# Linear attention layer: both batches in one program without a barrier, steps alternating on TensorE

## The chip, the cores and the metric

The program runs on one core of a Trainium2 chip. The metric is the device time of one execution in microseconds (us), lower is better. Three runs of the kernel before gave 1944.12, 1944.92 and 1945.78; their median is 1944.92 us. TensorE does the matrix products, VectorE (DVE) and ScalarE (ACT) the work on rows, GpSimd (POOL) and SyncE (SP) the rest. The engines run each its own list of instructions in order and wait for one another on semaphores only. Matmul results land in PSUM, which has eight banks of 512 float32 columns.

## The reference, cut to what matters

The program is a decoder of two blocks, six layers in all, on x of 2 x 1024 x 256 (batches, tokens, features). The change touches the first layer alone, linear attention with its feed-forward part. With 4 heads of 64 features it computes, for each batch by itself:

```
h1 = (x - mean) / sqrt(var + eps)                # a norm without gain
h2 = layer_norm(h1, ln1_g, ln1_b)                # a norm of the normed
q, k, v = h2 @ wq, h2 @ wk, h2 @ wv
q = softmax(q * scale) over the 64 features of a head
k = softmax(k * scale) over the 1024 tokens
context = k^T v  (64 x 64 for each head)
y = (q context) @ wo + bo + h1
y = gelu(layer_norm(y, ln2_g, ln2_b) @ w_ff1 + b_ff1) @ w_ff2 + b_ff2 + y
x = x + y @ w_d + b_d
```

All of it is in float32. w_ff1 is 256 x 1024 and w_ff2 1024 x 256, so these two hold half of the layer's products.

## The kernel before, in words

x lies in SBUF with features on partitions: two tiles of 128 features (k or m = 0, 1) and, for a batch, two halves of 512 tokens (j = 0, 1). `linear_attention_layer` runs a loop over the batches, `nc.Fori(0, B)` (L330), whose body is one block of four engine programs (L334). The block ends with a barrier of all engines. Both passes use the same `c.arena` of six slots, the same eight banks and the same semaphores, whose counts go on from pass to pass.

The order of work in a pass is written out by hand, as a list for each engine. TensorE (L349 on): the norm's mean and variance (`layer_norm_pe`: products with a matrix of 1/256), keys (L355, banks 0 to 3), values (L361, banks 4 to 7), queries (L368), the turned keys (transposes, L376), the contexts (L383), the turned queries (L390), attend (L397), the output projection (L403), the second norm, widening (L414, four banks in turn), narrowing (L422) and the last product (L430). ScalarE squares, takes logarithms and exponentials for the norm (`layer_norm_act`), the exponentials of keys (L440) and queries (L444), copies turned tiles out of PSUM (L447, L451, L456) and computes the gelu (L464). VectorE centres and scales (`layer_norm_dve`: L181, L185, L195, L201, L206), takes maxima of keys (L474), copies values (L481), shifts queries by their maximum (L487, L489), divides them by their sum (L493 to L497), copies the contexts (L508) and adds residuals (L514, L522, L528).

SyncE starts a transfer of one of two pieces of the later layers' weights in each pass (L340). After the loop `clear_signals` (L288) clears each semaphore of the layer on GpSimd, in a block of its own; `wait_for_weights` (L2372) is another, and then the next layer begins with the additions of L260.

Of the kernel before, what the change touches and what calls it, by code (L numbers as in the profile page):

```python
# [24 lines left out]
ALU = mybir.AluOpType  # L25
# [3 lines left out]
P = 128  # L29
B, S, D = 2, 1024, 256  # L30
T = B * S
FT = D // P
# [109 lines left out]
def layer_norm_pe(pe, c, s):  # L142

    for j in range(NCH):
        pe.wait_ge(*s["ln_sum"](j + 1))
        pe.matmul(c.bank(j), c.mean_w[:], c.ln_s[:, j, :], start=True, stop=True).then_inc(s["ln_mean"].sem)
    for j in range(NCH):
        pe.wait_ge(*s["ln_sq"](j + 1))
        for k in range(FT):
            mm = pe.matmul(c.bank(2 + j), c.mean_w[:], c.slot(3)[:, k, j * CH:(j + 1) * CH],  # L150
                           start=(k == 0), stop=(k == FT - 1))
        mm.then_inc(s["ln_var"].sem)


def layer_norm_act(act, c, s, twice=False):

    for j in range(NCH):  # L160
        act.wait_ge(*s["ln_cent"](j + 1))
        act.activation(c.slot(3)[:, :, j * CH:(j + 1) * CH], c.slot(2)[:, :, j * CH:(j + 1) * CH],
                       ACT.Square).then_inc(s["ln_sq"].sem)
    for j in range(NCH):
        act.wait_ge(*s["ln_var"](j + 1))
        ins = act.activation(c.ln_d[:, j, :], c.bank(2 + j), ACT.Ln, bias=c.eps[:, 0:1])
        if twice:
            ins = act.activation(c.ln_s[:, j, :], c.bank(2 + j), ACT.Ln, bias=c.eps_eps[:, 0:1], scale=1.0 + LN_EPS)
        ins.then_inc(s["ln_log"].sem)
    for j in range(NCH):  # L170
        act.wait_ge(*s["ln_log"](j + 1))
        ins = act.activation(c.ln_r[:, j, :], c.ln_d[:, j, :], ACT.Exp, scale=-0.5)
        if twice:
            ins = act.activation(c.ln_s[:, j, :], c.ln_s[:, j, :], ACT.Exp, scale=-0.5)
        ins.then_inc(s["ln_rstd"].sem)


def layer_norm_dve(dve, c, s, x, out, gain=None, bias=None, twice=False, once_out=None):

    for j in range(NCH):  # L180
        dve.tensor_tensor(c.ln_s[:, j, :], x(0, j), x(1, j), ALU.add).then_inc(s["ln_sum"].sem)  # L181
    for j in range(NCH):
        dve.wait_ge(*s["ln_mean"](j + 1))
        for k in range(FT):
            ins = dve.tensor_tensor(c.slot(2)[:, k, j * CH:(j + 1) * CH], x(k, j), c.bank(j), ALU.subtract)  # L185
        ins.then_inc(s["ln_cent"].sem)
    factor = c.ln_s if twice else c.ln_r
    for j in range(NCH):
        dve.wait_ge(*s["ln_rstd"](j + 1))
        centred = lambda k: c.slot(2)[:, k, j * CH:(j + 1) * CH]  # L190
        for k in range(FT):
            if gain is None:
                ins = dve.tensor_tensor(out(k, j), centred(k), factor[:, j, :], ALU.mult)
            else:
                ins = dve.scalar_tensor_tensor(out=out(k, j), in0=centred(k), scalar=gain(k), in1=factor[:, j, :],  # L195
                                               op0=ALU.mult, op1=ALU.mult)
                ins.then_inc(s["ln_scaled"].sem)
        if gain is not None:
            for k in range(FT):
                dve.wait_ge(*s["ln_scaled"](FT * j + k + 1))  # L200
                ins = dve.tensor_scalar(out(k, j), out(k, j), bias(k), None, ALU.add)  # L201
        if once_out is None or j < NCH - 1:
            ins.then_inc(s["ln_out"].sem)
        if once_out is not None:
            for k in range(FT):
                ins = dve.tensor_tensor(once_out(k, j), centred(k), c.ln_r[:, j, :], ALU.mult)  # L206
            if j == NCH - 1:
                ins.then_inc(s["ln_out"].sem)


LN_SIGNALS = {"ln_sum": NCH, "ln_mean": NCH, "ln_cent": NCH, "ln_sq": NCH, "ln_var": NCH, "ln_log": NCH, "ln_rstd": NCH,
              "ln_scaled": FT * NCH, "ln_out": NCH}
# [88 lines left out]
def linear_attention_layer(nc, c):  # L301

    DH = 64
    SCALE = float(DH) ** -0.25
    with ExitStack() as ctx:
        s = signals(nc, ctx, "a", dict(
            LN_SIGNALS, k_proj=4, k_max=4, k_shift=1, k_max_all=1, k_added=1, k_inv=1, zeroed=1, k_exp=4, k_turned=4, k_copied=4, v_proj=4, v_copied=4,
            q_proj=4, q_max=4, q_shift=4, q_exp=4, q_sum=4, q_inv=4, q_norm=4, q_turned=4, q_copied=4,
            ctx_done=1, ctx_copied=1, at_done=4, at_copied=4, o_done=4, y_done=4,
            ff_done=16, ff_gelu=16, f2_done=4, y2_done=4, d_done=4, x_done=4))  # L310
        s2 = signals(nc, ctx, "a2", LN_SIGNALS)
        sb = lambda name, shape: ctx.enter_context(nc.sbuf_tensor(name, shape, F32))
        k_mx = sb("a_k_mx", [P, FT, NCH])
        k_m = sb("a_k_m", [P, FT])
        k_s = sb("a_k_s", [P, FT, NCH])
        k_r = sb("a_k_r", [P, FT])
        q_m = sb("a_q_m", [P, 4, 8])
        q_s = sb("a_q_s", [P, 4, 8])
        context = sb("a_context", [P, FT, P])
        h1, h2, ek, v, ekt, qn = (c.slot(i) for i in range(6))  # L320
        v_t = v.rearrange("p a n -> p (a n)").rearrange("p (t n) -> p t n", t=TT)
        ekt_t = ekt.rearrange("p a n -> p (a n)").rearrange("p (t n) -> p t n", t=TT)
        q_t = qn.rearrange("p a n -> p (a n)").rearrange("p (u n) -> p u n", u=4)
        qt, at = c.slot(2), c.slot(5)
        y = h1
        hid = [c.arena[:, (2 + 2 * j) * 2048:(4 + 2 * j) * 2048].rearrange("p (f n) -> p f n", f=8) for j in range(NCH)]
# [3 lines left out]
        with nc.Fori(0, B) as b:  # L330
            set_round(b, s, s2)
            x = lambda k, j: c.xT[:, k, bass.ds(b * S + j * CH, CH)]
            col = lambda t: (lambda k, j: t[:, k, j * CH:(j + 1) * CH])
            with nc.Block() as block:  # L334

                @block.sync
                def _(sync):

                    sync.wait_ge(c.first_loaded, 32)
                    sync.dma_start(c.weights[:, bass.ds(b * part + n_first, part)],  # L340
                                   c.weights_dram[:, bass.ds(b * part + n_first, part)]).then_inc(c.others_loaded, 16)

                @block.gpsimd
                def _(pool):
                    pool.memset(context[:], 0.0).then_inc(s["zeroed"].sem)

                @block.tensor
                def _(pe):
                    layer_norm_pe(pe, c, s)  # L349
                    pe.wait_ge(c.first_loaded, 32)  # L350
                    pe.wait_ge(*s["ln_out"](NCH))
                    for m in range(FT):
                        for j in range(NCH):
                            for k in range(FT):
                                mm = pe.matmul(c.bank(2 * m + j), c.w("a_wk", k, m * P, P), h2[:, k, j * CH:(j + 1) * CH],  # L355
                                               start=(k == 0), stop=(k == 1))
                            mm.then_inc(s["k_proj"].sem)
                    for u in range(4):
                        for t in (0, 1):
                            for k in range(FT):  # L360
                                mm = pe.matmul(c.bank(4 + u)[:, t * D:(t + 1) * D], h2[:, k, (2 * u + t) * P:(2 * u + t + 1) * P],  # L361
                                               c.w("a_wv", k, 0, D), start=(k == 0), stop=(k == 1))
                        mm.then_inc(s["v_proj"].sem)
                    for u in range(4):
                        pe.wait_ge(*s["v_copied"](u + 1))
                        for t in (0, 1):
                            for k in range(FT):
                                mm = pe.matmul(c.bank(4 + u)[:, t * D:(t + 1) * D], h2[:, k, (2 * u + t) * P:(2 * u + t + 1) * P],  # L368
                                               c.w("a_wq", k, 0, D), start=(k == 0), stop=(k == 1))
                        mm.then_inc(s["q_proj"].sem)  # L370

                    pe.wait_ge(*s["k_exp"](4))
                    for u in range(4):
                        for t in (0, 1):
                            for m in range(FT):
                                mm = pe.transpose(c.bank(u)[:, t * D + m * P:t * D + (m + 1) * P],  # L376
                                                  ek[:, m, (2 * u + t) * P:(2 * u + t + 1) * P], c.ident[:])
                        mm.then_inc(s["k_turned"].sem)
# [29 lines left out]
                    for j in range(NCH):  # L408
                        pe.wait_ge(*s2["ln_out"](NCH))
                        for f in range(8):  # L410
                            if n >= 4:
                                pe.wait_ge(*s["ff_gelu"](n - 3))
# [2042 lines left out]
```

## Time and profile before

| what | value |
|---|---|
| median of three runs | 1944.92 us |
| the profiled execution | 1944.75 us |
| its span, first to last instruction | 1943.0 us |
| mean granted TensorE clock | 0.938 |
| TensorE, VectorE, ScalarE busy | 1688.1, 941.2, 625.1 us |
| first pass of the layer, from the first addition to the second pass's | 7.7 to 155.9 us |
| second pass, to the last addition | 155.9 to 301.8 us |
| next layer's first addition | 306.95 us |

The rows further down come from the one profiled execution. A float32 matmul with 512 columns shows as two records, so 64 records of L414 are 32 matmuls. A row of a timeline may merge several instructions in succession ("x8"); its second number is then the time from the first's start to the last's end. The granted clock is 1.0 at 2.4 GHz and 0.5 at 1.2 GHz.

### The profile page before, as it was taken

The numbers are of one execution on the slowest core, as the hardware profiler recorded it, in microseconds if no ns is written. First come the engines' busy times: TensorE is split into PE (matmuls) and PEld (weight loads), VectorE is DVE, ScalarE is ACT, GpSimd is POOL, SyncE is SP. The second block draws the span as 40 slices with busy tenths as digits, with TensorE's granted clock in tenths as the row PEclk, the third lists the DMA queues.
The fourth block names the chain that finished last, engine by engine and source line by source line (L and its number), as shares of the span: only waits on it lengthen the run. The fifth ranks groups of instructions, "written<-read, shape, count | busy, mean of one in ns | idle before, by whom it ended". The sixth has DMA issues, their size and how long they took to land. (4 is left out here: it accounts for less than half of the span.)

```text
span 1943.0 us, 19762 instructions
## 1 busy us (share of the span) xinstructions
PE 1688.1 (87%) x7458; PEld 955.6 (49%) x7458; DVE 941.2 (48%) x1490; ACT 625.1 (32%) x1024; POOL 119.4 (6%) x92
## 2 busy tenths in 40 slices
PE   5796795989999958977799999778767999999998
PEld 3443442543222213333444544345553888888886
DVE  3404404567656541133587775355545536353542
ACT  2312322432232231114166666242242222221220
POOL 0000000001121200003500000000011000000000
PEclk8898897989999979988899999899968999999999
DMA  4001000000000000002724520000111022222211
GB/s 174 0 0 59 0 0 4 0 1 1 1 1 1 1 1 0 0 0 76 87 82 52 67 34 2 3 1 0 52 36 58 1 87 87 87 87 87 87 30 44
DMA packets 27693, 67.47 MB, mean 35 GB/s; under 512 B 3096, under 2 KB 14424, under 8 KB 25176
## 3 DMA queue, kind: packets, MB, share of 16 engines
q1 hardware_dynamic: 27608, 66.33, 12.5%
q8 instruction: 54, 0.88, 0.2%
q14 instruction: 31, 0.25, 0.0%
HBM read 57.80 MB, written 8.39 MB: 34 GB/s over the span
## 5 line engine op out<-in xcount | busy, mean ns | idle before, releaser
L1566 ACT ACTIVATE arena<-psum 128x512 f32<-128x512 f32 (+3 forms) x384 | 164.3, 499 | 123.6 <-PE psum L1470 91.6
L1606 DVE TENSOR_REDUCE b_mx<-psum 128x1 f32<-128x512 f32 (+3 forms) x304 | 181.5, 653 | 45.0 <-PE psum L1448 34.4
L2100 PE MATMUL psum<-m_wo,m_hidden 128*128 128x256 f32 (+1 forms) x704 | 153.4, 379 | 1.0 <-DVE arena L2303 1.0
L2198 ACT ACTIVATE m_gelu<-psum 128x512 f32<-128x512 f32 (+1 forms) x88 | 52.6, 598 | 305.1 <-PE psum L2086 305.1
L2100 PEld LDWEIGHTS psum<-m_wo,m_hidden 128*128 128x128 f32 (+1 forms) x704 | 133.3, 190 | 19.7 <-issue 1.2
L2086 PE MATMUL psum<-m_x_high,m_w_high 128*128 128x512 f32 (+1 forms) x352 | 139.9, 398 | 2.9 <-issue 2.9
L2086 PE MATMUL psum<-m_x_rest,m_w_high 128*128 128x512 f32 (+1 forms) x352 | 138.8, 394 | 0.0
L2086 PE MATMUL psum<-m_x_high,m_w_rest 128*128 128x512 f32 (+1 forms) x352 | 138.4, 393 | 0.0
L2322 DVE TENSOR_TENSOR m_hidden<-m_gelu,psum 128x512 f32<-128x512 f32 (+1 forms) x88 | 60.5, 688 | 139.8 <-PE psum L2086 139.8
L878 ACT ACTIVATE x_probs<-psum 128x1024 f32<-128x1024 f32 x64 | 65.5, 1024 | 179.4 <-PE psum L734 179.4
L954 DVE TENSOR_REDUCE x_mx<-psum 128x2 f32<-128x1024 f32 x64 | 77.4, 1222 | 83.6 <-PE psum L708 82.4
L1467 PE MATMUL psum<-b_q_stack,b_k_stack 98*128 98x512 bf16 (+3 forms) x288 | 91.4, 334 | 7.4 <-DMA b_q_stack<-b_stage 3.0
L1445 PE MATMUL psum<-b_k_stack,b_q_stack 96*128 96x512 bf16 (+3 forms) x288 | 90.2, 345 | 6.0 <-POOL weights_sb L1395 3.7
L747 PE MATMUL psum<-x_probs,arena 128*64 128x512 f32 x256 | 69.5, 621 | 6.8 <-ACT x_out L888 6.8
L2086 PEld LDWEIGHTS psum<-m_x_high,m_w_high 128*128 128x128 f32 (+1 forms) x352 | 65.0, 185 | 19.9 <-issue 3.7
L734 PE MATMUL psum<-arena 64*128 64x512 f32 x256 | 73.7, 653 | 0.0
L2086 PEld LDWEIGHTS psum<-m_x_high,m_w_rest 128*128 128x128 f32 (+1 forms) x352 | 65.0, 185 | 16.5
L2086 PEld LDWEIGHTS psum<-m_x_rest,m_w_high 128*128 128x128 f32 (+1 forms) x352 | 65.0, 185 | 16.3
L1482 PE MATMUL psum<-arena,weights_sb 128*32 128x512 f32 (+3 forms) x768 | 71.7, 492 | 0.0
L414 PE MATMUL psum<-arena,weights_sb 128*128 128x512 f32 x128 | 58.5, 620 | 14.2 <-DVE arena L201 14.2
L708 PE MATMUL psum<-arena 64*128 64x512 f32 x256 | 68.1, 623 | 3.1 <-DVE x_mx L954 1.9
L1132 PE MATMUL psum<-weights_sb 128*128 x96 | 48.9, 634 | 18.1 <-PEq L1110 12.2
(372 smaller groups left out, 2730.8 us busy)
## 6 DMA issues: line engine op xcount, KB each, us to landing
m_w<-w SPq DMA_DIRECT2D x16, 1368.0 KB, 8.9
m_wo<-wo SPq DMA_DIRECT2D x8, 1280.0 KB
weights_sb<-weights SPq DMA_DIRECT2D x2, 2820.0 KB, 8.9
b_q_stack<-b_q_dram SPq DMA_DIRECT2D x36, 128.0 KB, 6.9
b_k_stack<-b_k_dram SPq DMA_DIRECT2D x36, 128.0 KB, 7.4
weights_sb<-weights SPq DMA_DIRECT2D x1, 3328.0 KB, 13.0
b_q_dram<-b_q_parts SPq DMA_DIRECT2D x6, 512.0 KB, 3.3
b_k_dram<-b_k_parts SPq DMA_DIRECT2D x6, 512.0 KB, 4.4
```

The costliest lines, as they stand in the source:

```text
L708: mm = pe.matmul(to[:, h * CH:(h + 1) * CH], qt[b][rows, m, q0:q0 + P], kt_[b][rows, m, first:first + CH], start=True, stop=True)
L734: mm = pe.matmul(to[0:keys, h, :], k, qt[b][rows, m, half * CH:(half + 1) * CH], start=False, stop=True)
L747: mm = pe.matmul(out_tile[h * DH:(h + 1) * DH, :], v, probs[slot % RING][0:keys, h, :], start=(kt == 0), stop=(kt == TT))
L878: ins = act.activation(probs[slot % RING][:], two_heads(units), ACT.Exp, scale=SCALE)
L954: dve.tensor_reduce(mx[:, n % 2, i // 2, i % 2, :], two_heads(tile(("piece", n, i))), AX, ALU.max).then_inc(s["read"].sem)
L1445: mm = pe.matmul(bank[:, x * keys:(x + 1) * keys], qs[n % 3][0:ROWS, h, qi * P:(qi + 1) * P], ks[n % 3][0:ROWS, h, first:first + keys], st ...
L1467: mm = pe.matmul(score(slot)[:, 0:n], ks[a][0:ROWS + SHIFT, h, ki * P:(ki + 1) * P], qs[a][0:ROWS + SHIFT, h, q0:q0 + n], start=True, stop ...
L1482: mm = pe.matmul(out_tile[h * PAD:(h + 1) * PAD, CH - n:CH], v_aug[:, b * TT + ki, quad * QUAD + h, :], probs[(QUAD * (2 * pair + i) + h) ...
L1566: act.activation(probs[slot % RING][:, 0:n], score(slot)[:, 0:n], ACT.Exp, scale=SCALE).then_inc(s["expd"].sem)
L1606: dve.tensor_reduce(mx[:, part, qi, heads[0]:heads[0] + nh], tile(("piece", p))[:, 0:nh * keys].rearrange("p (h n) -> p h n", n=keys), AX, ...
L2086: mm = pe.matmul(c.bank(base + n % 2)[0:H_N(h), :], of[:, k, at], x_of[:, k, :], start=(k == 0 and of is w_high[w] and x_of is x_high), st ...
L2100: mm = pe.matmul(bank[:, q * D:(q + 1) * D], hidden[0:H_N(h), h, (2 * i + q) * P:(2 * i + q + 1) * P], wo[0:H_N(h), h, :], start=(h == 0), ...
```

## The change

The loop goes. The Python code writes both batches into one block, with no barrier between them. Batch b has semaphores, an arena (a second one of 48 KB per partition is added), small tables and four banks of its own (4b to 4b + 3). The three layer norm helpers go; their steps become small functions of the batch, as do all others. Each engine's program is a list of such steps in which the batches alternate. Within the steps:

- The first norm's factor that h2 needs is exponentiated first; the other (`once`) has its own signal, and h1 is computed after h2. The keys start once the first half of h2 is there.
- With four banks, values and queries use the keys' banks: values wait for the exponentials of the keys, the turned keys for the shifted queries. The turned queries have three banks in turn, since the fourth holds the contexts; the widening has two in turn.
- Projection, second norm and narrowing go half by half of the tokens.
- SyncE starts both pieces of weights at once. The clears go over the semaphores of both batches.

The core of the diff (steps with the same body as before are left out):

```diff
-        with nc.Fori(0, B) as b:
-            set_round(b, s, s2)
...
+        arenas = (c.arena, sb("a_arena", [P, 6 * FT * S]))
...
+        bank = lambda b, i: c.bank(4 * b + i)
+        turn_bank = lambda b, u: bank(b, u % 3)
...
+                for i in range(B):
+                    at_i = slice(n_first + i * part, n_first + (i + 1) * part)
+                    sync.dma_start(c.weights[:, at_i], c.weights_dram[:, at_i]).then_inc(c.others_loaded, 16)
...
+                def by_token(b, name, free, done):
+                    for u in range(4):
+                        pe.wait_ge(*free(u + 1))
...
+                def turn_queries(b):
+                    for u in range(4):
+                        pe.wait_ge(*sg[b]["q_norm"](u + 1))
+                        if u == 3:
+                            pe.wait_ge(*sg[b]["q_copied"](1))
...
+                def widen(b, j):
+                    pe.wait_ge(*ln2[b]["out"](j + 1))
+                    for f in range(8):
+                        if f >= 2:
+                            pe.wait_ge(*sg[b]["ff_gelu"](8 * j + f - 1))
...
+                def narrow(b, j):
+                    pe.wait_ge(*sg[b]["ff_gelu"](8 * (j + 1)))
...
-        clear_signals(nc, s, s2)
+        clear_signals(nc, *ln1, *ln2, *sg, also=[zeroed])
```

The three lists, one step after another (in the diff each is one line of code, `ln1`, `ln2` the two norms' signals):

```
TensorE: mean(0, ln1) variance(0, ln1) [first weights] keys(0) mean(1, ln1) values(0)
  variance(1, ln1) queries(0) keys(1) turn_keys(0) values(1) contexts(0) queries(1)
  turn_queries(0) attend(0) turn_keys(1) project(0) contexts(1) turn_queries(1)
  mean(0, ln2) attend(1) variance(0, ln2) project(1) widen(0, 0) mean(1, ln2) widen(0, 1)
  variance(1, ln2) narrow(0, 0) widen(1, 0) narrow(0, 1) last(0, 0) widen(1, 1) last(0, 1)
  narrow(1, 0) narrow(1, 1) last(1, 0) last(1, 1)
ScalarE: square(0) roots_twice(0) exp_keys(0) square(1) roots_twice(1) exp_queries(0)
  exp_keys(1) copy_keys(0) exp_queries(1) copy_queries(0) copy_attended(0) copy_keys(1)
  copy_queries(1) square(0, ln2) copy_attended(1) roots(0) gelus(0, 0) square(1, ln2)
  gelus(0, 1) roots(1) gelus(1, 0) gelus(1, 1)
VectorE: add_halves(0) centre(0) [first weights] add_halves(1) normalise(0)
  normalise_once(0) max_keys(0) centre(1) copy_values(0) normalise(1) shift_queries(0)
  normalise_once(1) max_keys(1) copy_values(1) normalise_queries(0) copy_context(0)
  shift_queries(1) normalise_queries(1) add_attended(0) centre(0, ln2) copy_context(1)
  normalise(0, ln2) add_attended(1) centre(1, ln2) normalise(1, ln2) add_narrow(0, 0)
  add_narrow(0, 1) add_last(0, 0) add_narrow(1, 0) add_last(0, 1) add_narrow(1, 1)
  add_last(1, 0) add_last(1, 1)
```

## Rows read from the trace of the kernel before

**Rows 1.** The page's totals: engine, busy us (share of the span) xinstructions.
```profile
PE 1688.1 (87%) x7458; PEld 955.6 (49%) x7458; DVE 941.2 (48%) x1490; ACT 625.1 (32%) x1024; POOL 119.4 (6%) x92
```
**Rows 2.** Table of stretches: its length, each engine's busy us, PEclk, DMA share, GB/s.
```profile
27.60:90.50 62.90, 48.68 (x180) 31.33 (x180) 29.83 (x54) 18.91 (x32) 0.00 (x0) 0.91 0.00 0
...
155.00:238.00 83.00, 54.80 (x193) 33.84 (x194) 40.33 (x72) 30.10 (x46) 0.31 (x1) 0.89 0.09 35
...
7.70:155.90 148.20, 119.63 (x336) 61.87 (x336) 46.44 (x80) 41.84 (x63) 0.36 (x2) 0.93 0.11 44
```
**Rows 3.** Timeline, norm to keys in both passes: start, us, work, [idle before <-releaser].
```profile
17.88 138.23 SPq L340 DMA_DIRECT2D weights_sb<-weights  x2
...
19.56 0.63 ACT L172 ACTIVATE ln<-ln 128x512 f32<-128x512 f32 x1
...
20.74 1.41 DVE L195 SCALAR_TENSOR_TENSOR arena<-arena,vectors_sb,ln 128x512 f32<-128x512 f32 x2 [7.32 <-ACT ln L174]
...
22.86 1.28 DVE L206 TENSOR_TENSOR arena<-arena,ln 128x512 f32<-128x512 f32 x2
24.07 1.41 DVE L195 SCALAR_TENSOR_TENSOR arena<-arena,vectors_sb,ln 128x512 f32<-128x512 f32 x2
...
27.62 9.42 PE L355 MATMUL psum<-arena,weights_sb 128*128 128x512 f32 x16 [10.90 <-DVE arena L206]
...
155.92 1.29 DVE L181 TENSOR_TENSOR ln<-xT 128x512 f32 x2 [0.95 <-PEq L334]
...
160.26 3.70 PE L150 MATMUL psum<-arena,mean_w 128*128 128x512 f32 x8 [1.61 <-ACT arena L162]
...
167.76 1.41 DVE L195 SCALAR_TENSOR_TENSOR arena<-arena,vectors_sb,ln 128x512 f32<-128x512 f32 x2 [7.45 <-ACT ln L174]
```
**Rows 4.** Timeline of TensorE in the first pass.
```profile
36.87 7.07 PE L361 MATMUL psum<-weights_sb,arena 128*128 128x256 f32 x32
...
50.69 1.91 PE L376 MATMUL psum<-ident,arena 128*128 128x128 f32 x16
...
54.97 5.46 PE L383 MATMUL psum<-arena 128*128 128x128 f32 x32 [2.37 <-ACT arena L447]
...
67.48 7.13 PE L403 MATMUL psum<-arena,weights_sb 128*128 128x512 f32 x16 [0.69 <-ACT arena L456]
...
90.55 29.29 PE L414 MATMUL psum<-arena,weights_sb 128*128 128x512 f32 x64 [7.08 <-DVE arena L201]
...
119.68 27.63 PE L422 MATMUL psum<-arena,weights_sb 128*128 128x512 f32 x64
```
**Rows 5.** The clears of one line, and the next layer's first work in the timeline.
```profile
L288 POOLq EVENT_SEMAPHORE_RANGE_CLEAR  x51: 44/44/48, 302.2 to 306.1; - x51
...
306.95 2.50 DVE L260 TENSOR_TENSOR ln<-xT 128x512 f32<-128x512 f32 x4 [5.14 <-PEq L2372]
```
**Rows 6.** Table of stretches, one us among the contexts.
```profile
57.00:58.00 1.00, 1.00 (x7) 1.00 (x6) 0.93 (x3) 0.00 (x0) 0.00 (x0) 0.50 0.00 0
```
**Rows 7.** Timeline of TensorE in the next layer.
```profile
402.32 3.73 PE L696 MATMUL psum<-x_k_diag,arena 128*128 128x128 f32 x32
```
**Rows 8.** Timeline of VectorE and ScalarE in the first pass.
```profile
37.08 0.69 DVE L474 TENSOR_REDUCE a_k_mx<-psum 128x1 f32<-128x512 f32 x1 [1.02 <-PE psum L355]
...
38.78 0.19 ACT L440 ACTIVATION_READ_ACCUMULATOR arena<-psum,a_k_m 128x1 f32 x1
...
51.62 0.69 DVE L489 TENSOR_TENSOR arena<-psum,a_q_m 128x512 f32<-128x512 f32 x1
52.22 0.68 DVE L493 TENSOR_REDUCE a_q_s<-arena 128x8 f32<-128x512 f32 x1
...
53.78 0.68 DVE L493 TENSOR_REDUCE a_q_s<-arena 128x8 f32<-128x512 f32 x1
...
60.58 1.18 DVE L508 TENSOR_SCALAR a_context<-psum,a_k_r 64x64 f32<-64x64 f32 x4 [1.77 <-PE psum L383]
...
95.85 0.69 ACT L464 ACTIVATE arena<-psum,vectors_sb 128x512 f32<-128x512 f32 x1 [1.03 <-PE psum L414]
```

More of the change, by code:

```diff
@@ L155, in layer_norm_act @@
[L155 to L175, printed above, removed]
@@ L178, in layer_norm_dve @@
[L178 to L208, printed above, removed]
@@ L329, in linear_attention_layer, with _, mean, variance @@
         assert n_first + B * part == c.weights.shape[1]
-        with nc.Fori(0, B) as b:
-            set_round(b, s, s2)
[L332 to L353, printed above, removed]
+        with nc.Block() as block:
+            @block.sync
+            def _(sync):
+                sync.wait_ge(c.first_loaded, 32)
+                for i in range(B):
+                    at_i = slice(n_first + i * part, n_first + (i + 1) * part)
+                    sync.dma_start(c.weights[:, at_i], c.weights_dram[:, at_i]).then_inc(c.others_loaded, 16)
+            @block.gpsimd
+            def _(pool):
+                pool.memset(context[:], 0.0).then_inc(zeroed)
+            @block.tensor
+            def _(pe):
+                def mean(b, s):
+                    for j in range(NCH):
+                        pe.wait_ge(*s["sum"](j + 1))
+                        pe.matmul(bank(b, 2 * j), c.mean_w[:], factor(b, j), start=True, stop=True).then_inc(s["mean"].sem)
+                def variance(b, s):
+                    for j in range(NCH):
+                        pe.wait_ge(*s["sq"](j + 1))
+                        for k in range(FT):
+                            mm = pe.matmul(bank(b, 2 * j + 1), c.mean_w[:], squares[b][:, k, col(j)], start=(k == 0), stop=(k == 1))
+                        mm.then_inc(s["var"].sem)
+                def keys(b):
+                    for j in range(NCH):
+                        pe.wait_ge(*ln1[b]["out"](j + 1))
+                        for m in range(FT):
@@ L372, in _, with values, queries @@
-                    pe.wait_ge(*s["k_exp"](4))
-                    for u in range(4):
+                                mm = pe.matmul(bank(b, u)[:, t * D:(t + 1) * D], h2[b][:, k, (2 * u + t) * P:(2 * u + t + 1) * P],
+                                               c.w(name, k, 0, D), start=(k == 0), stop=(k == 1))
+                        mm.then_inc(done.sem)
+                def values(b):
+                    by_token(b, "a_wv", sg[b]["k_exp"], sg[b]["v_proj"])
+                def queries(b):
+                    by_token(b, "a_wq", sg[b]["v_copied"], sg[b]["q_proj"])
@@ new lines, in turn_queries, with attend, project @@
+                        mm.then_inc(sg[b]["q_turned"].sem)
+                def attend(b):
+                    pe.wait_ge(*sg[b]["ctx_copied"](1))
+                    pe.wait_ge(*sg[b]["q_copied"](4))
+                    for j in range(NCH):
+                        for m in range(FT):
+                            pe.matmul(bank(b, 2 * j + m), context[:, b, m, :], qt[b][:, m, col(j)],
+                                      start=True, stop=True).then_inc(sg[b]["at_done"].sem)
+                def project(b):
+                    for j in range(NCH):
+                        pe.wait_ge(*sg[b]["at_copied"](2 * (j + 1)))
@@ L435, in _ @@
[L435 to L441 removed]
+                            mm.then_inc(sg[b]["o_done"].sem)
@@ new lines, in widen @@
+                def widen(b, j):
[3 more added lines that the diff above has]
+                            pe.wait_ge(*sg[b]["ff_gelu"](8 * j + f - 1))
+                        for k in range(FT):
+                            mm = pe.matmul(bank(b, 2 * j + f % 2), c.w("a_w1", k, f * P, P), h2[b][:, k, col(j)],
+                                           start=(k == 0), stop=(k == 1))
+                        mm.then_inc(sg[b]["ff_done"].sem)
@@ new lines, in _ @@
+                mean(0, ln1[0])
+                variance(0, ln1[0])
+                pe.wait_ge(c.first_loaded, 32)
+                keys(0)
+                mean(1, ln1[1])
+                values(0)
+                variance(1, ln1[1])
+                queries(0)
+                keys(1)
+                turn_keys(0)
+                values(1)
+                contexts(0)
+                queries(1)
+                turn_queries(0)
+                attend(0)
+                turn_keys(1)
+                project(0)
@@ new lines, in _ @@
+                contexts(1)
+                turn_queries(1)
+                mean(0, ln2[0])
+                attend(1)
+                variance(0, ln2[0])
+                project(1)
+                widen(0, 0)
+                mean(1, ln2[1])
+                widen(0, 1)
+                variance(1, ln2[1])
+                narrow(0, 0)
+                widen(1, 0)
+                narrow(0, 1)
+                last(0, 0)
+                widen(1, 1)
+                last(0, 1)
+                narrow(1, 0)
```

419 lines of the change are left out of this document (251 added, 168 removed).

## The prediction, made before the changed kernel ran

> **What bounds the kernel now.** I read the totals of the page first [rows 1]: TensorE is busy for 87% of the span, so what is to be had lies where it is not. The table of stretches finds such a place in this layer [rows 2]: between 27.6 and 90.5 us TensorE has matmuls for 48.7 of 62.9 us and they run at a mean granted clock of 0.91; in the second pass of the loop, 155 to 238 us, for 54.8 of 83.0. The order in time says why: a batch is one chain through three engines (matmul, then VectorE or ScalarE, then matmul), and nothing else is there to run meanwhile. The layer norm ahead of the keys leaves TensorE idle for 10.9 us, the keys' first records are at half rate, the contexts wait 2.4 us for ScalarE's copies, and the wide matmuls 7.1 us for the second norm [rows 3, 4]. From there on the pass is dense: 64 records of L414 and 64 of L422 follow one another. The first pass runs from 7.7 to 155.92 us, the second to 301.81 (next work at 306.95 after 5.14 us idle) [rows 3, 5]. These 294.1 us are what the change acts on.
>
> **The least that TensorE needs.** At full rate a float32 matmul with 512 columns (two records) takes 27.63 x 2 / 64 = 0.86 us; 32 records with 256 columns 6.9 (7.07 less the tail of the last); 16 transposes 1.9 [rows 4]. The contexts' 32 records took 5.46, but at half rate for most of it [rows 4, 6]; 32 records of the same size at full rate took 3.73 in the next layer [rows 7], so I take 3.7. One batch then is: mean 1.7, variance 3.45, keys, values and queries 6.9 each, keys turned 1.9, contexts 3.7, queries turned 1.9, attend 3.45, projection 6.9, second mean and variance 5.15, widening and narrowing 27.5 each, last 6.9: 110.75 us. The total is 221.5, as before: no matmul is added or removed.
>
> **Part 1: the start.** Batch 0's first norm has no companion yet and stays as it is until ScalarE's exponentials. The factor that the keys need is now exponentiated first, so it is there at about 20.2 (the first one started at 19.56), where the second was waited for until 20.74. The second output of the norm (1.21 us per half) moves behind, and the keys start after half of the columns: scaling and bias of a half take 22.86 - 20.74 = 2.12 us [rows 3]. The keys start at 22.4 instead of 27.6. VectorE waits here for the first weights and for batch 1's x; they are there at 17.88, when SyncE issues what waits for them, 2 us before VectorE is needed [rows 3], so I cost that at nothing; were it later, each us would be one of the whole. TensorE still idles for some 6 us ahead, so I keep the half-rate start: 16 records took 9.42 where 7.13 is full [rows 3, 4], 2.4 us.
>
> **Part 2: where TensorE still waits.** I walked the three written orders, each engine in its order, with the durations of before.
> - Keys(0) end at 31.7, mean(1) at 33.4. Values now reuse the keys' banks and wait for the exponentials: from the last maximum's start to the first sum read is 1.9 us (37.08 to 38.97) [rows 8]. 0.4 idle.
> - Values(0) to 40.7, variance(1) to 44.1, queries(0) to 51.0, keys(1) to 57.9, keys(0) turned to 59.8: no wait. But VectorE gets batch 1's factor only at 47.65 (variance's start to first scaling was 160.26 to 167.76, one exponential less now) [rows 3], and has queued behind it: normalise(1) 4.25, shift_queries(0) 4 x (0.73 + 0.61), normalise_once(1) 2.4, then the maxima of keys(1) at 0.61 each [rows 3, 8]. The first exponential of keys(1) is ready at 63.4. Idle 3.6 us.
> - Values(1) to 72.1 (with the clock's loss, below), contexts(0) 75.8, queries(1) 82.7. VectorE copies values(1) to 73.0, normalises the queries of 0 (1.56 per quarter: 6.25), copies the context (1.18 [rows 8], and an estimated 0.4 for the two small operations ahead) and shifts the queries of 1: 86.2; ScalarE's exponential of the last quarter (0.65) ends at 86.85, and only behind it stand the copies of turned queries(0). The turned queries have three banks instead of four, so the fourth quarter waits for the first copy (87.4), and attend(0) for the last (88.7). Idle 3.3 + 0.8 = 4.1.
> - Attend(0), keys(1) turned, projection(0), contexts(1), queries(1) turned and the second mean(0) run without a wait to 110.05. The copy of context(1) stands on VectorE behind the centring of batch 0: attend(1) starts at 113.45. Idle 3.4.
> - Attend(1), variance(0), projection(1) to 129.05; the factor for batch 0 is there at 125.0 and h2's first half at 127.2, under projection(1). From here on the other batch covers each norm: roots(1) and normalise(1) need about 7.5 us and lie under narrow(0, 0), 13.75. The widening has two banks instead of four; the gelu of a step runs 0.2 + 0.69 us after its matmuls while the next step takes 1.72 [rows 8], so it fits; only squares(1) ahead of the second half's gelus costs 0.3.
>
> Sum of idle: 0.4 + 3.6 + 4.1 + 3.4 + 0.3 = 11.8 us.
>
> **Part 3: the clock.** After an idle gap of 2.37 us the contexts came to a granted clock of 0.50, the 1.2 GHz level (57 to 58 us [rows 6]); after gaps of 0.69 and 1.61 the records of L403 and of the second pass's variance (8 in 3.70) took no longer than at full rate [rows 3, 4]. I take that each of my three gaps over 3 us does the same: 5.46 - 3.7 = 1.8 us each, 5.4 in all. Bounds: nothing, if the level holds, and 2.4 each (the keys' loss). The contexts themselves are spared it.
>
> A rule of the Trainium skill speaks against interleaving here: "TensorE: Matmul & The Clock Gate", section "A second HAM failure mode: psum-queue depth-cycling", has a kernel that cycles its PSUM banks, idles for moments between groups of matmuls and so swings between the two rates. By the rows only the gaps over 2 us do so; by the page each handing over of a bank could, which is the rival on the slow side below.
>
> **Part 4: around it.** The program clears each semaphore of the layer behind a barrier: 51 clears from 302.2 to 306.1, 0.078 us each [rows 5]. Now there are 2 x 11 + 2 x 9 + 2 x 32 + 1 = 105: 54 more, 4.2 us on the path, because nothing else runs there. The second piece of weights (2820 KB) is issued with the first at 18 us, not at 156; no work of the layer waits for it, and it takes no queue that another needs then: 0, at most 1 us should VectorE or TensorE be slowed by it. The loop's barrier and branch go: the idle at the pass change is in the 294.1 already. Memory of its own for batch 1 costs no instruction. ScalarE's table loads become no more than they were, and those on a norm's chain are in its 7.5 us.
>
> **The sum.** TensorE from the start of keys(0): 221.5 - 5.15 = 216.35. Then 22.4 + 216.35 + 11.8 idle + 2.4 + 5.4 clock + 0.8 (the last addition) = 259.15 us for the layer's end, where it was 301.81: 42.65 less. With 4.2 for the clears 38.45 remain. The profiled execution took 1944.75 (span 1943.0), 0.17 below the median, so the forecast is 1944.75 - 38.45 = 1906.3 us.
>
> **Rivals.**
> A. TensorE bound almost throughout: the three gaps are not there since I overstate VectorE's queue. Then 11.1 and 5.4 us go: 1889.8. For it: VectorE works for 46.4 us in a pass and TensorE for 119.6 [rows 2], so the mean load leaves room. Against it: engines run in order, and the three waits come from what stands ahead in the order, not from load. 5%.
> B. The fewer banks bind: 32 widening steps and 8 quarters wait for ScalarE. Were each of the 32 handings over 0.2 us late, 6.4 us: 1912.7. Against it the margin of 0.8 us. 6%.
> C. More waits in the attention part than I found, each with its clock loss: two more of 3.5 + 1.8 us: 1916.9. For it: in this part nearly every step has a partner on another engine that is itself queued. 8%.
> D. Slower: the clock stays at 0.50 through the interleaved part, because small waits are now everywhere in it. Between keys(0) and the widening lie 87.4 us of matmuls; all at half rate would give 1906.3 + 87.4 - 7.8 = 1985.9. It decides the sign once 38.45 + 7.8 = 46 of these 87 us run at half rate. Against it: L403 at full rate right after its gap of 0.69 us [rows 4]. 2%.
> E. The change doesn't interleave (some wait of batch 1 falls on the end of batch 0): then only the clears and the start (5.2 us for each pass at best) count, 1944.75 + 4.2 - 10.4 to 1949: about 1944. 1%.
> The forecast itself has 78%: it varies by the bounds of the clock (1900.9 to 1908.1) and by 3 us for the walk's rounding and waits.
>
> The range that should hold 8 in 10: from 1899 (part of A) to 1916 (B and most of C). What can be told from no change is 0.2%, 3.9 us: faster 0.96 (forecast, A, B, C), same 0.015, slower 0.025 (D, part of E).
>
> **What would show it.** In the changed kernel's profile: keys(0) at 22.4; TensorE idle before values(1), around the last quarter of turned queries(0) and before attend(1), 3 to 4 us each, released by ScalarE, ScalarE and VectorE, with a granted clock near 0.5 behind each; no gap over 0.5 us from the first widening matmul (near 129 us) to the last addition (259); 105 clears over 8.2 us; the next layer's first addition near 269. Wrong would be: a half-rate stretch in the widening, gelus that TensorE waits for, waits for the first weights on VectorE, or a next layer that takes another time than before.

## The result

Four executions of the changed kernel took 1907.13, 1908.17, 1914.15 and 1915.57 us, median 1911.16; four of the kernel before 1944.12 to 1945.78, median 1944.83. The ratio is 0.9826 (95% interval 0.981 to 0.9841): 1.7% faster. The forecast was 1906.3 with a range of 1899 to 1916. The profiled execution took 1907.13 us.

| | before | after, profiled |
|---|---|---|
| span | 1943.0 | 1905.4 |
| first layer's last addition ends | 301.8 | 258.9 |
| clears | 51, 302.2 to 306.1 | 105, 259.2 to 266.9 |
| next layer's first addition | 306.95 | 267.75 |
| from there to the end of the span | 1636.05 | 1637.65 |

So the first layer and its clears give 39.2 us, and the later layers, whose code is the same, take 1.6 us back in this execution.

TensorE's timeline of the changed kernel through the interleaved part (start, us, work, idle before and its releaser; L322 values and queries, L313 keys, L337 turned keys, L345 contexts, L356 turned queries, L365 attend, L373 projection, L299 and L305 mean and variance, L383 widening):

```profile
12.79 3.70 PE L305 MATMUL psum<-arena,mean_w 128*128 128x512 f32 x8 [0.92 <-ACT arena L446]
22.34 8.53 PE L313 MATMUL psum<-arena,weights_sb 128*128 128x512 f32 x16 [5.86 <-DVE arena L558]
30.71 1.88 PE L299 MATMUL psum<-ln,mean_w 128*128 128x512 f32 x4
32.87 7.17 PE L322 MATMUL psum<-weights_sb,arena 128*128 128x256 f32 x32 [0.27 <-ACT arena L475]
...
57.09 1.91 PE L337 MATMUL psum<-ident,arena 128*128 128x128 f32 x16
62.44 8.86 PE L322 MATMUL psum<-weights_sb,a_arena 128*128 128x256 f32 x32 [3.44 <-ACT a_arena L475]
71.13 3.73 PE L345 MATMUL psum<-arena 128*128 128x128 f32 x32
...
81.61 1.47 PE L356 MATMUL psum<-ident,arena 128*128 128x128 f32 x12
86.45 0.90 PE L356 MATMUL psum<-ident,arena 128*128 128x128 f32 x4 [3.37 <-ACT arena L494]
88.13 6.34 PE L365 MATMUL psum<-arena,a_context 128*128 128x512 f32 x8 [0.78 <-ACT arena L494]
94.30 1.91 PE L337 MATMUL psum<-ident,a_arena 128*128 128x128 f32 x16
96.05 7.03 PE L373 MATMUL psum<-arena,weights_sb 128*128 128x512 f32 x16
...
108.39 1.88 PE L299 MATMUL psum<-ln,mean_w 128*128 128x512 f32 x4
113.47 5.40 PE L365 MATMUL psum<-a_arena,a_context 128*128 128x512 f32 x8 [3.20 <-DVE a_context L612]
118.70 3.60 PE L305 MATMUL psum<-arena,mean_w 128*128 128x512 f32 x8
122.14 7.03 PE L373 MATMUL psum<-a_arena,weights_sb 128*128 128x512 f32 x16
129.00 13.90 PE L383 MATMUL psum<-arena,weights_sb 128*128 128x512 f32 x32
```

The reader is to see that the waits of 10.90, 2.37 and 7.08 us of [rows 3, 4] are gone: where one batch's norm or copies run, the row in between belongs to the other batch (`arena` is batch 0, `a_arena` batch 1). Three gaps over 3 us remain, and behind each the same work takes longer than it has to: 8.86 us for what takes 7.17 at 32.87, 6.34 and 5.40 for attend, 3.60 at full rate. The contexts at 71.13 take 3.73 where they took 5.46 [rows 4].

The table of stretches of the changed kernel shows the clock behind these three gaps, and the feed-forward part (length, busy us of PE, PEld, DVE, ACT, POOL, PEclk, DMA share, GB/s):

```profile
63.00:66.00 3.00, 3.00 (x8) 2.37 (x8) 0.05 (x1) 3.00 (x9) 0.00 (x0) 0.50 0.00 0
...
90.00:92.00 2.00, 2.00 (x4) 0.97 (x3) 1.33 (x3) 0.68 (x2) 0.00 (x0) 0.50 0.00 0
...
115.00:117.00 2.00, 2.00 (x4) 0.87 (x3) 0.00 (x0) 0.78 (x2) 0.00 (x0) 0.50 0.00 0
...
129.00:251.00 122.00, 122.00 (x285) 53.88 (x284) 19.23 (x30) 30.36 (x41) 0.00 (x0) 1.00 0.00 0
```

From 129 to 251 us TensorE has work all the time at a granted clock of 1.00. In the kernel before each pass entered this part from a wait of 7.08 us and began it at a lowered clock: L414 took 29.29 us where L422, with as many matmuls, took 27.63 [rows 4].

The clears and what follows them, a line's rows and VectorE's timeline:

```profile
L222 POOLq EVENT_SEMAPHORE_RANGE_CLEAR  x105: 44/44/48, 259.2 to 266.9; - x105
```
```profile
258.17 0.75 DVE L634 SCALAR_TENSOR_TENSOR xT<-psum,vectors_sb,xT 128x512 f32<-128x512 f32 x1 [0.97 <-PE psum L399]
267.75 2.50 DVE L194 TENSOR_TENSOR ln<-xT 128x512 f32<-128x512 f32 x4 [8.83 <-PEq L2511]
```

A clear is 0.044 us long but comes every 0.074 (7.7 us over 104 steps), and VectorE stands idle for 8.83 us where it was 5.14 [rows 5].

### The profile page after: what moved, and what is told of

It is laid out like the page before. It is cut to its first block and busy times, and to the rows that moved or that the text cites. A ratio compares the mean times of both kernels' runs of the same rounds, so it can differ in the third digit from the quotient of the medians.

```text
span 1905.4 us, 19665 instructions
## 1 busy us (share of the span) xinstructions
PE 1683.0 (88%) x7458; PEld 952.8 (50%) x7458; DVE 939.4 (49%) x1490; ACT 623.4 (33%) x1023; POOL 119.1 (6%) x91
## 5 line engine op out<-in xcount | busy, mean ns | idle before, releaser
L2225 PEld LDWEIGHTS psum<-m_x_high,m_w_rest 128*128 128x128 f32 (+1 forms) x352 | 65.0, 185 | 16.5
L179 ACT ACTIVATE arena<-arena 128x1024 f32<-128x1024 f32 x20 | 21.1, 1057 | 140.4 <-DVE arena L198 139.8
```

What stands on the lines that cost most here:

```text
L2225: mm = pe.matmul(c.bank(base + n % 2)[0:H_N(h), :], of[:, k, at], x_of[:, k, :], start=(k == 0 and of is w_high[w] and x_of is x_high), st ...
```

## The experiments

All medians are of five runs (fill: four), each beside nine or ten of the kernel before on the same chip. Three chips were used: again, serial, gaps and ranges ran on one (kernel before: median 1945.61), fill, late22, late44 and best on a second (1946.52), best2 and best_fill on a third (1945.74). So a comparison across the first two chips carries some 0.9 us that are not the changed kernel's. What is said of a stretch or a gap comes from one profiled execution of each run.

**again: the changed kernel once more.** 

> The changed kernel itself, unaltered, to see where its executions differ: four of them took 1907.1, 1914.2, 1908.2 and 1915.6 us, those of the kernel before 1944.1 to 1945.8. Theory (clock): the layer's short waits of about 3.3 us leave it open whether TensorE's clock is lowered behind them, so the same program takes 1907 to 1916 us, and the profile of a longer execution shows its 7 us as lower granted clock and longer matmuls behind gaps. Rival (a wait in data movement or in the code's loading): all stretches at the same clock, and one gap of several us on SyncE, VectorE or TensorE that the profile of 1907 us does not have. Median expected 1908 to 1914.

Measured: 1907.94 to 1916.32, median 1910.4. The first layer is the same (next layer's first addition at 267.68). The profiled execution's later layers took 1641.0 us. I took the starts of the same instructions on GpSimd, and of that addition, in each trace, and subtracted. In us, by stretch of the later layers (A two stretches, the next layer's norm and its first products; B its middle; C its end and the recurrent layer; D the causal one; E the context one; F and G the experts):

```
              A      A      B       C       D       E      F      G      all
before         25.04  99.02  232.16  233.06  348.89  155.53  51.40  490.95  1636.1
after          25.75  96.41  232.15  232.41  349.59  158.39  51.75  491.20  1637.7
again          25.69  96.92  232.17  235.81  349.21  158.22  51.74  491.26  1641.0
late22         25.08  98.99  232.17  233.14  348.89  155.53  51.50  490.94  1636.2
late44         24.32  98.59  232.18  236.40  348.72  158.77  51.56  490.90  1641.4
gaps           25.80  96.44  232.16  232.42  349.62  156.99  50.25  494.54  1638.2
```

B, where TensorE is busy for 224 of 232 us at a clock of 1.00, is constant to 0.03 us; the others differ from execution to execution, by up to 4 us. (The code of these layers is the same in all six; serial and fill belong here too, with 1640.5 and 1642.3 us in all.) What differs inside C is seen in TensorE's timeline, first of the profiled changed kernel, then of again:

```profile
653.88 5.07 PE L906 MATMUL psum<-weights_sb 128*128 128x512 f32 x8 [4.27 <-DVE weights_sb L1132]
665.75 5.97 PE L168 MATMUL psum<-ln,mean_w 128*128 128x512 f32 x8 [6.81 <-DVE ln L194]
```
```profile
653.99 6.62 PE L906 MATMUL psum<-weights_sb 128*128 128x512 f32 x8 [4.27 <-DVE weights_sb L1132]
667.42 6.75 PE L168 MATMUL psum<-ln,mean_w 128*128 128x512 f32 x8 [6.81 <-DVE ln L194]
```

The same gap of 4.27 us costs the matmuls behind it 1.6 us more in one execution than in the other. That the rest of C goes the same way is seen in its row of the table of stretches, again first of the profiled changed kernel:

```profile
622.06:854.47 232.41, 181.50 (x420) 72.84 (x421) 65.52 (x85) 57.52 (x74) 15.03 (x10) 0.88 0.00 0
```
```profile
622.46:858.27 235.81, 184.81 (x420) 74.06 (x421) 65.76 (x85) 57.81 (x74) 15.03 (x10) 0.86 0.00 0
```

C is 3.40 us longer, and TensorE's busy time in it is 3.31 us longer for the same 420 records, at a lower mean clock: its idle time hardly changed. Over all later layers TensorE is busy for 1450.9 and 1453.8 us, 2.9 of the 3.4 us. So between these two executions the difference is the clock's, lowered for longer or shorter behind the same gaps, and not a new wait; the rival falls for them. In the first layer too: again's values(1) after the same 3.43 us took 7.17 us, not 8.86, while its keys(0) took 10.11, not 8.53. The longest executions, 1914 to 1916 us, were not profiled, and the nearest to them that was, late44's, is taken up below.

**serial: no interleaving.** PE's, ScalarE's and VectorE's lists hold all steps of batch 0, then of batch 1:

```diff
                 keys(0)
-                mean(1, ln1[1])
                 values(0)
-                variance(1, ln1[1])
                 queries(0)
-                keys(1)
                 turn_keys(0)
-                values(1)
                 contexts(0)
-                queries(1)
                 turn_queries(0)
                 attend(0)
+                project(0)
+                mean(0, ln2[0])
...
```

> The new program with its steps, arenas, banks and semaphores, but each engine's list does all of batch 0 first and then all of batch 1: no interleaving. Theory (the other batch's matmuls fill the waits): nearly all of the gain goes; what is left is the earlier start of the keys (5.3 us in each batch), less 4 us for 54 more clears and some us for banks that are fewer, so 1933 to 1945 us. Rival (the gain comes from the finer steps and the loop that went): it stays near 1911, at most 1920.

Measured: 1936.65 to 1941.38, median 1938.87; the next layer's first addition at 299.25 after the same 8.82 us for the clears. TensorE's timeline ahead of the keys and the widening of batch 1:

```profile
162.98 9.76 PE L313 MATMUL psum<-a_arena,weights_sb 128*128 128x512 f32 x16 [5.54 <-DVE a_arena L558]
...
194.62 5.47 PE L345 MATMUL psum<-a_arena 128*128 128x128 f32 x32 [1.96 <-ACT a_arena L487]
...
225.88 29.43 PE L383 MATMUL psum<-a_arena,weights_sb 128*128 128x512 f32 x64 [4.96 <-DVE a_arena L558]
```

The waits are back: 5.54, 1.96 and 4.96 us, where the old code had 10.67 to 10.90, 2.37 and 7.08. The layer ends at 290.4 against 301.8 before: 11.4 us come from the finer steps (keys and widening start after half of the tokens, the needed factor first) and the loop that went, less what the four banks cost: in each batch the values now wait 1.99 us for the exponentials of the keys, a wait that the old code with eight banks did not have. Interleaving gives 299.25 less 267.7, 31.6 us, between these two profiles, and 28.5 us between the medians of serial and again. 2.4 of the 31.6 are not its work: serial's first variance, ahead of any interleaving, took 6.11 us in its profile and 3.70 in again's. By either number the rival (finer steps alone, at most 1920 us) falls.

**gaps: three swaps of neighbours.**

```diff
-                normalise_once(1)
                 max_keys(1)
+                normalise_once(1)
...
-                exp_queries(1)
                 copy_queries(0)
+                exp_queries(1)
...
-                centre(0, ln2[0], of_y)
                 copy_context(1)
+                centre(0, ln2[0], of_y)
```

> Three swaps of neighbours in the written orders: VectorE takes the maxima of keys(1) ahead of normalise_once(1) and copies context(1) ahead of centring batch 0's y; ScalarE copies the turned queries(0) ahead of the exponentials of queries(1). Theory (the three waits come from what is queued ahead on VectorE and ScalarE): the gaps of 3.44, 3.37 + 0.78 and 3.20 us go, and with them 1.8, 2.7 and 1.8 us of lowered clock: 17 us less than the changed kernel at the same clock, about 1890 to 1892 (1889.8 was rival A of the prediction), and the executions agree within 2 us. Rival (those engines are simply full): new waits of the same sum take their place, less than 5 us are gained.

Measured: 1893.73 to 1896.34, median 1893.89, 16.5 us under again. TensorE's timeline at the three places:

```profile
62.00 7.17 PE L322 MATMUL psum<-weights_sb,a_arena 128*128 128x256 f32 x32 [1.02 <-ACT a_arena L475]
...
82.40 3.67 PE L365 MATMUL psum<-arena,a_context 128*128 128x512 f32 x8 [0.84 <-ACT arena L494]
...
101.72 3.60 PE L365 MATMUL psum<-a_arena,a_context 128*128 128x512 f32 x8
```

The gaps are 1.02, 0.84 (which was there) and none, and all work behind them runs at full rate. The median is 2 us above the 1890 to 1892 expected, and the executions differ by 2.6 us, not within 2. The next layer begins at 254.18, 13.5 us earlier than in again, not 17: in both of these profiles keys(0) took 10.1 us, again had lost nothing behind the first gap, and 1.0 us of that gap stays. VectorE and ScalarE were not full; they did things in the wrong order. Rival A of the prediction put a kernel without the three gaps at 1889.8; another order reaches most of that.

**ranges: clears by range**, in all six layers:

```diff
-            for sem in [sig.sem for group in groups for sig in group.values()] + list(also):
-                pool.sem_clear(sem)
+            nums = sorted(getattr(sem, "num") for sem in [sig.sem for group in groups for sig in group.values()] + list(also))
...
+                if at + 1 == len(nums) or nums[at + 1] != n + 1:
+                    pool.sem_clear(range(first, n + 1))
```

> The changed kernel, but the clears at each layer's end are done by range: one instruction for each run of neighbouring semaphore numbers in place of one for each semaphore, in all six layers (283 clears of 0.074 us in all become some 6 to 12). Theory (the clears lie on the path, since nothing else runs between the layers): 105 x 0.074 = 7.8 us less at the end of the first layer, and 20.5 us less in all: 1887 to 1895. Rival (a range clear takes as long as its single clears): no change within 2 us. Rival (the clears of later layers are hidden): only 7.8 us less.

Measured: 1892.94 to 1894.26, median 1893.38, 17.0 us under again. All the clears of the program are now eight instructions; a line's rows and VectorE's timeline at the end of the first layer:

```profile
L225 POOLq EVENT_SEMAPHORE_RANGE_CLEAR  x8: 86/163/612, 260.5 to 1891.0; - x8
```
```profile
261.90 2.50 DVE L194 TENSOR_TENSOR ln<-xT 128x512 f32<-128x512 f32 x4 [1.66 <-PEq L2515]
```

105 semaphores take 0.612 us in one instruction, and VectorE's idle time falls from 8.82 to 1.66: 7.2 us in the first layer, as reckoned within 0.6. The later layers take 1629.5 us in place of 1637.7 to 1641.0, 8.2 to 11.5 less; their 171 fewer clears would be 12.7. So most of them lie on the path there too; the remainder is no larger than what the later layers differ by from execution to execution. Both rivals fall.

**fill: matmuls that nobody reads, in two gaps.** They use a free bank; nothing of the result changes.

```diff
+                            if b == 0:
+                                pe.wait_ge(*sg[b]["ctx_copied"](1))
+                                idle_work(3)
                             pe.wait_ge(*sg[b]["q_copied"](1))
...
                 mean(0, ln2[0])
+                idle_work(3)
                 attend(1)
```

> The changed kernel with three matmuls of 128 x 512 whose result nobody reads (a full matrix product each, 0.86 us, into bank 3 of batch 0, which is free then) in each of two gaps: before the last quarter of turned queries(0) and before attend(1). The waits stay, TensorE is only kept at work in them. Theory (the half-rate matmuls behind a gap come from TensorE's idling, not from what runs there): attend(0) takes 3.6 in place of 6.2 to 6.3 us, attend(1) 3.6 in place of 5.4, so the first layer ends 4.4 us earlier, near 254.5, and the next begins near 263.3. Rival (those matmuls are slow for their own operands or for ScalarE's reads of PSUM beside them): they keep 6.2 and 5.4 us, and the layer ends at 258.9 or later.

Measured: TensorE's timeline of fill (L298 the added matmuls, L372 attend):

```profile
82.96 2.74 PE L298 MATMUL psum<-weights_sb,mean_w 128*128 128x512 f32 x6
...
87.95 3.67 PE L372 MATMUL psum<-arena,a_context 128*128 128x512 f32 x8 [0.90 <-ACT arena L502]
...
107.27 2.74 PE L298 MATMUL psum<-weights_sb,mean_w 128*128 128x512 f32 x6
...
110.63 3.70 PE L372 MATMUL psum<-a_arena,a_context 128*128 128x512 f32 x8 [0.62 <-DVE a_context L620]
```

The same attend with the same operands takes 3.67 and 3.70 where it took 6.34 and 5.40, at a granted clock of 1.00 (82 to 92 and 110 to 115 us), and the next layer begins at 263.21, 4.5 us earlier. This is no chance of one execution: in all five profiles in which the gaps stand unfilled (the changed kernel, again, ranges, late22, late44) attend(0) took 6.21 to 6.70 and attend(1) 5.40. So the loss behind these two gaps is caused by TensorE's idling: shown. The median of 1906.65 (1905.04 to 1907.28) is 3.8 under again's, 4.7 with the 0.9 between the chips. The profiled execution itself took 1907.22 us, because its later layers took 1642.3.

**late22 and late44: a delay between the layers.**

```diff
-        clear_signals(nc, *ln1, *ln2, *sg, also=[zeroed])
+        clear_signals(nc, *ln1, *ln2, *sg, also=[zeroed] * 23)   # late44: 45
```

> The changed kernel with 22 clears more at the end of the first layer (they clear one semaphore again), 1.6 us of delay between the first and the second layer and nothing else. It asks where the spread of 1907 to 1916 us comes from; so far the first layer ended at the same 258.9 us in two executions whose later layers took 1637.7 and 1641.0 us. Theory (how a later idle gap falls in the clock's course decides its loss): the delay moves all later gaps, and median and spread change otherwise than by 1.6 us: by more than 2 us off 1912.0, or to a spread under 3 us. Rival (chance in each execution alone): median 1912 within 2 us and the same spread of 8 us.

> As late22 with 44 clears more, 3.3 us of delay. Theory (clock's course): again not on the line through 1910.4 and a slope of one; a kernel with a delay could even be no slower than the changed kernel. Rival (chance alone): 1913.7 within 2 us, spread 8 us.

Measured: late22 1908.98 to 1915.46, median 1912.1; late44 1910.47 to 1916.65, median 1916.2, with four of five runs within 1.2 us. Again, from which the line was drawn, ran on the other chip; with the 0.9 us between the chips the line of a plain delay passes through 1912.9 and 1914.6. late22 lies 0.8 below it and late44 1.6 above, both within the 2 us of the rival, and their spreads of 6.5 and 6.2 us are near again's 8.4. So five runs each give no support to the theory, and they don't refute it. The delay was not the only shift either: in both profiled executions the first layer ended some 2.5 us later, because variance(0) took 6.10 and 6.09 us after a gap of 0.76 us, where it took 3.70 after the same gap in ranges and best2. Whether a fixed shift picks the levels of later layers stays open. late44's profile, of its longest execution (1916.65 us), is 9.5 us longer than the changed kernel's: 3.3 are the delay, 2.6 the first layer, 3.7 the later ones (1641.4 us). Without the delay such steps alone would make it 1913 us.

**best: swaps and ranges together.** 

> The three swaps (run gaps: 13.5 us earlier into the next layer than the changed kernel, median 1893.9) and the clears by range (run ranges: median 1893.4) together. Theory (they act in different places, waits inside the layer and the stretch between layers): both gains add up, 1893.4 less 13.5 to 16.5: 1877 to 1880 us. Rival (part of each gain is a shift of where the later layers' gaps fall in the clock's course): the sum misses by 3 us or more, to either side.

> The run best once more, on the same chip as best_fill, to compare the two and to see which of two lengths each later layer's stretch takes: median 1875 within 2 us, the first layer's end where it was (next addition at 246.9, at most 1.7 later or earlier with the clock at keys(0)).

Measured: best 1871.52 to 1876.33, median 1875.07; best2, the same kernel on another chip, 1871.32 to 1873.96, median 1871.93; ratios 0.9625 (0.9612 to 0.9638) and 0.9624 (0.9611 to 0.9637) to the kernel before. Adding both gains gave 1877 to 1880; in best's profile the next layer begins at 246.93, which is 254.18 less 7.2, so in the first layer they add up, though with a variance(0) of 5.89 us where gaps had 3.70 and keys(0) of 8.67 where it had 10.12. The later layers take 1627.7 and 1624.4 us in the two profiles. The sum is missed by 2 to 5 us (3 to 6 with the 0.9 between the chips), to the fast side; the rival asked for 3 or more, so it is near the line between the two. best2 missed its own expectation, 1871.93 for 1875 within 2, while its next layer began at 245.60, within the 1.7 us allowed. This is the fastest version I ran: 3.8% below the kernel before, where the changed kernel (again) is 1.8% below it.

**best_fill: five unread matmuls ahead of keys(0).**

```diff
                 pe.wait_ge(c.first_loaded, 32)
+                for i in range(5):
+                    pe.matmul(bank(1, 3), c.mean_w[:], c.w("a_w1", 0, 0, CH), start=True, stop=True)
```

> The run best with five matmuls of 128 x 512 whose result nobody reads between the first weights' arrival (about 18 us) and the start of keys(0) (22.4 us), 4.3 us in all. Theory (TensorE's idling ahead of the keys causes the half rate; in the run fill two other gaps lost theirs so): keys(0) take 7.0 in place of 8.5 to 10.1 us, values(0) and all behind them come 1.5 to 3 us earlier, the next layer's first addition near 244.5 in place of 246.93; the median 1872 to 1873.5. Rival (the added matmuls push the keys or are slow themselves, because TensorE has idled 1 us before them as well): 246.9 or later.

Measured: median 1877.8 (1875.8 to 1880.12), 5.9 us above best2. TensorE's timeline of best_fill (L411 the added matmuls):

```profile
13.35 6.22 PE L309 MATMUL psum<-arena,mean_w 128*128 128x512 f32 x8 [0.76 <-ACT arena L452]
19.41 4.46 PE L411 MATMUL psum<-weights_sb,mean_w 128*128 128x512 f32 x10
25.11 7.13 PE L317 MATMUL psum<-arena,weights_sb 128*128 128x512 f32 x16 [1.25 <-DVE arena L564]
```

keys(0) run at full rate, 7.13 us, as the theory said; but in this profile the variance ahead had taken 6.22 us, as it took 5.89 to 6.11 in best, serial and both late runs without any filler, so the keys started at 25.11 and the next layer at 246.42. best2, with a variance of 3.70, had 245.60; best, with 5.89, had 246.93. The expectation (244.5, a median of 1872 to 1873.5) is missed, and the rival's 246.9 or later is not reached either. Most of the 5.9 us is in the later layers (1629.7 against 1624.4). As a gain it is a miss; as evidence on the clock it agrees with fill: in no profile without the filler did keys(0) take under 8.51 us.

## Why the prediction was right

**Part 1, the start:** keys(0) forecast at 22.4, measured 22.34. Cost of the half-rate start 2.4; measured 8.53 less 7.13, 1.4, and 3.0 in again.

**Part 2, the waits:** forecast 0.4, 3.6, 3.3 + 0.8, 3.4 and 0.3 us, released by ScalarE, ScalarE, ScalarE and VectorE; measured 0.27, 3.44, 3.37 + 0.78, 3.20, and 0.21 within the second widening. The swaps show that the cause is what stands ahead in the lists. The walk's later marks: attend(1) 113.45, measured 113.47; widening 129.05, measured 129.00; last addition 259.15, measured 258.92. That is closer than its terms deserve, and this is luck: the clock's terms were 1.0 us too large at the keys and 0.9 too small behind the gaps.

**Part 3, the clock:** 1.8 us for each of three gaps, 5.4; measured 8.86 less 7.17, 6.34 less 3.67 and 5.40 less 3.70, with 0.2 at the last quarter: 6.3 us. The bounds of 0 and 2.4 were too tight above (2.7 behind two gaps with a short piece of work between) and right below (none in again). Of the rule in "TensorE: Matmul & The Clock Gate" of the Trainium skill, section "A second HAM failure mode: psum-queue depth-cycling", nothing is seen here: the widening hands over two banks in turn, and the 122 us in which it lies run at 1.00. TensorE idles there for 0.21 us at most, so this is no test of a kernel that does idle between its groups. Rival D with its 46 us at half rate was far off.

**Part 4, around it:** 54 more clears 4.2 us; measured 3.7. VectorE's wait for batch 1's x, costed at nothing, did cost nothing, but nearly. Its timeline in the changed kernel:

```profile
18.17 1.29 DVE L541 TENSOR_TENSOR ln<-xT 128x512 f32<-128x512 f32 x2 [4.98 <-DMA xT<-x_t]
19.99 1.42 DVE L554 SCALAR_TENSOR_TENSOR arena<-arena,vectors_sb,ln 128x512 f32<-128x512 f32 x2 [0.53 <-ACT ln L458]
```

The wait ended at 18.17, and two additions of batch 1 came behind it ahead of batch 0's scaling. What was left is 0.53 us, not 2; the prediction had not counted those 1.3 us of additions.

**Rivals:** A did not come, since the three gaps were there; B (banks) cost nothing beyond the 0.21; C's two further waits don't exist; E is refuted by serial.

**What was off:** the sum put all later layers at their old length. In the profiled execution they took 1.6 us more, which with 39.2 gained in place of 38.45 gives 1907.13 against 1906.3. That this execution comes so near is partly luck: it is the shortest of the four. The median of 1911.2 lies 4.9 us above the forecast, inside the range, and shows the term I left out. Executions of the changed kernel differ by 8 us; those of the old one by 2.8 (ten, on again's chip), 6.0 and 3.8 (nine each, on the two others). Profiles show where such steps lie: 1637.7 and 1641.0 us in the later layers, and in the first layer 1.6 us at keys(0), 1.7 at values(1) and 2.4 at variance(0). Which of them made the two executions over 1914 us is not shown, as they were not profiled. The prediction named a next layer that takes another time among what would prove it wrong, and gave it no us. The Trainium skill has it in "TensorE: Matmul & The Clock Gate", section "What's actually happening": the clock's monitor runs free of the kernel's start, so one kernel gets its full rate at different places; the levels above are consistent with it, but late22 and late44 did not decide it. Whether the changed kernel spreads more than the one before is not sure either.

## What to carry to other kernels

When a stage is one chain across engines, give it a second independent chain with banks and buffers of its own and write both into the same lists; here that was worth 28 to 32 us of 290. Then read each remaining gap from its releaser's own queue: three swaps of neighbours gave another 13.5 us, waits and clock together. And look at what runs between the stages: clearing semaphores one by one cost as much here (17.0 us between the medians, 7.2 of them in this layer) as the waits that the swaps removed.

## What the hardware showed that I had not expected

- The same gap gives different losses in executions of the same program: 7.17 or 8.86 us for the same values(1) after 3.4 us, 5.07 to 6.71 for L906 after 4.27. The first variance, after 0.76 us, took 3.70 in ranges and best2 and 5.89 to 6.22 in five others, best among them, whose code is best2's; the table of stretches reads a clock of 1.00 there in both cases, so the rows don't show why. A profile of one execution gives a level, not an average.
- Matmuls that nobody reads, 2.74 us of them in a wait, bring back up to 2.7 us behind it. They are no cure for a wait: the swaps gave 13.5 us over three waits where the fill gave 4.5 in two of them.
- A range clear of 105 semaphores takes 0.612 us, single ones 0.074 each.
